# Expert rows summed into the residual inside the expert phase, by VectorE and GpSimd in turn

## What is computed

```python
x = x + xattn(ctx_768, layernorm(x), mask)
h = layernorm(x)
topk_idx, topk_w = route(h)                       # 4 of 32 experts per token
mixed  = sum over the 4 of  topk_w * down_e(silu(gate_e(h)) * up_e(h))
shared = shared_down(silu(shared_gate(h)) * shared_up(h))
x = x + mixed + shared
```

## Time and profile before

| | us |
|---|---|
| median of three runs (lowest, highest) | 1342.62 (1340.92, 1345.98) |
| the profiled execution | 1343.46 |
| its span, first to last instruction | 1341.5 |
| busy in the span: TensorE | 1298.0 (97%) |
| busy: ScalarE | 1011.6 (75%) |
| busy: VectorE | 972.0 (72%) |
| busy: GpSimd | 643.4 (48%) |

### The profile page before, as it was taken

How to read it: one execution, slowest core, us unless ns; L and a number is a source line. 1 busy time by engine, 2 the same in 40 slices (tenths; PEclk the granted TensorE clock), 3 DMA queues, 4 the chain that set the end, 5 groups by cost and what they waited for, 6 DMA issues and landing times.

```text
span 1341.5 us, 32944 instructions
## 1 busy us (share of the span) xinstructions
PE 1298.0 (97%) x8718; PEld 1043.2 (78%) x8718; DVE 972.0 (72%) x4498; ACT 1011.6 (75%) x2730; POOL 643.4 (48%) x724
## 2 busy tenths in 40 slices
PE   6999999999999999999979899999999999999997
PEld 4566676676676766766658799999999999988886
DVE  4578898888988988888887455555555555548887
ACT  4899999999999999999851566766776676653332
POOL 1113555555555555555455366666666666640000
PEclk8999999999999999999989899999999999999999
DMA  8234645535545445454487655555655555438896
GB/s 278 84 133 136 205 162 176 192 131 187 176 138 190 161 153 195 136 179 162 168 304 246 194 169 172 172 172 168 178 169 174 169 173 166 132 114 313 304 319 218
DMA packets 147714, 247.14 MB, mean 184 GB/s; under 512 B 24139, under 2 KB 110413, under 8 KB 146896
## 3 DMA queue, kind: packets, MB, share of 16 engines
q1 hardware_dynamic: 121472, 177.63, 41.3%
q0 software_dynamic: 26064, 67.42, 14.5%
HBM read 104.68 MB, written 119.96 MB: 167 GB/s over the span
## 4 chain that ended last, share of the span: by engine, by line
PE 63%; ACT 21%; DVE 9%; issue 5%; DMA 2%; SPq 0%; POOL 0%; ACTq 0%; DVEq 0%
PE psT L1033 10%; PE ps L1033 9%; PE psS L1043 9%; ACT arena L1168 6%; PE ps L916 6%; PE ps L1024 5%; PE ps L852 4%; ACT arena L1160 4%; PE psS L927 3%; PE psT L827 3%; PE psS L813 3%; PE psO L840 2%; ACT arena L1128 2%; ACT arena L1132 2%; ACT arena L1175 2%
## 5 line engine op out<-in xcount | busy, mean ns | idle before, releaser
L701 POOL DMA_INDIRECT expert_out<-pay,dest x287 | 282.1, 983 | 175.1 <-DVE dest L1878 157.4
L556 POOL DMA_INDIRECT lists<-pay,slot x168 | 174.3, 1037 | 187.7 <-PE psT L827 39.6
L1043 PE MATMUL psS<-arena,history 128*128 x574 | 171.8, 381 | 0.3 <-DVE history L1865 0.3
L1033 PEld LDWEIGHTS ps<-pad,hist_j 128*128 128x128 f32 x1152 | 152.1, 193 | 9.5 <-ACT pad L1315 2.1
L1033 PEld LDWEIGHTS psT<-pad 128*128 128x128 f32 x1144 | 151.0, 192 | 7.3
L1033 PE MATMUL ps<-pad,hist_j 128*128 128x128 f32 x1152 | 152.8, 276 | 1.9 <-ACT pad L1315 1.9
L1033 PE MATMUL psT<-pad 128*128 128x128 f32 x1144 | 151.6, 276 | 0.0
L1872 DVE TENSOR_SCALAR pay<-psS,dest 128x256 f32<-128x256 f32 x287 | 138.9, 484 | 1.6 <-PE psS L1043 1.5
L757 PE MATMUL ps<-arena 128*128 128x512 f32 x256 | 128.3, 624 | 2.6 <-ACT arena L1120 2.0
L556 POOL DMA_INDIRECT lists<-arena,slot x88 | 91.0, 1034 | 79.4 <-PE psT L827 20.6
L1168 ACT ACTIVATE arena<-arena,rden 128x256 f32<-128x256 f32 x256 | 109.1, 503 | 15.2 <-DVE rden L1466 15.1
(11 more groups left out here) (238 smaller groups left out, 3284.1 us busy)
## 6 DMA issues: line engine op xcount, KB each, us to landing
lists<-pad SPq DMA_DIRECT2D x72, 516.0 KB, 5.2
pay<-lists SPq DMA_DIRECT2D x287, 129.0 KB, 2.2
arena<-expert_out SPq DMA_DIRECT2D x32, 1024.0 KB, 7.1
pay<-pay SPq DMA_DIRECT2D x42, 384.0 KB, 3.6
x<-in_x SPq DMA_DIRECT2D x32, 256.0 KB, 4.7
out<-arena SPq DMA_DIRECT2D x31, 256.0 KB, 5.8
arena<-arena SPq DMA_DIRECT2D x20, 384.0 KB, 3.4
arena<-in_ctx SPq DMA_DIRECT2D x32, 192.0 KB, 4.6
```

What stands on the lines that cost most here:

```text
L556: pool.indirect_dma_start(lists, bass.IndirectOffsetOnAxis(ap=slots(u)[:, j, k:k + 1], axis=0), paid(u)[:, j, k, :], None).then_inc(scat[3 ...
L701: pool.indirect_dma_start(expert_out, bass.IndirectOffsetOnAxis(ap=dest[:, t % DESTS, 1:2], axis=0), yy[n], None, bounds_check=T * TOPK - ...
L1033: m = pe.matmul(ps[2 + n % 2][:, which * P:(which + 1) * P], w_now[1 - n % 2][:, k, which * I:(which + 1) * I], xsT[:, n % 2, k * P:(k + 1 ...
L1043: pe.matmul(dbank[n % 2][:, 0:D], hh[:, n % 4, :], w_dn[:, at(e, 1), :].rearrange("p a n -> p (a n)"), start=True, stop=True)\
```

## The change

In the expert phase, from tile 55 on, SP loads one piece for every two tiles: for one block of 128 tokens two of the four expert rows of each token (256 KB) into `side`, which has three buffers. VectorE adds the first row of the piece to `x1` in place (`add_first`, behind `weigh_result` of every second tile), and then GpSimd adds the second (`add_second`, behind a scatter). VectorE's add waits for the piece and for GpSimd's add of the piece before; GpSimd's waits for VectorE's of the same piece. 116 pieces cover the first 29 units (`IN_PHASE`); the last three are summed in the last stage as before, now into `x1`. The first eight units are stored during the expert phase; the others are stored from `x1` as their shared part is added, and `res` is gone. `n1T` is saved in HBM for all 32 units, and the last stage loads it into a ring of four instead of normalising and transposing again; `mr`, `norm_again`, `shared_turn` and `turned` are gone. The masks and `bo_b` move into `side`, which is free in the attention stage.

```diff
-ER_DEPTH = 4
+PIECES = 3
+IN_PHASE = 29
+PIECE_LOAD, PIECE_ADD = 55, 53
+N1T_RING = 4
...
+        side = sb("side", [P, PIECES, 2 * D])
+        mask_u8 = side[:, 0, 0:D].bitcast(u8).rearrange("p (a j n) -> p a j n", a=4, j=2)
+        mask_row = side[:, 0, D:2 * D].bitcast(bf16).rearrange("p (a j n) -> p a j n", a=2, j=2)
+        bo_b = side[:, 1, 0:D]
...
         def n1T_of(u):
-            flat = early_n1T[:, u] if u < EARLY else late_set[1]
+            flat = early_n1T[:, u] if u < EARLY else side[:, 0, :] if u == EARLY else n1T_ring[(u - EARLY - 1) % N1T_RING]
...
-                if (s + -2).exists() and s.n - 2 < EARLY:
+                if (s + -2).exists():
                     save_n1T(s + -2)
...
             load_experts(above, below_wo)
             spread_rows(Unit(UNITS // 2 - 1, 0))
-
+            save_n1T(Unit(UNITS // 2 - 1, 0))
 
             sp.wait_ge(y_done, NB)
             load_experts(below_wo, E)
             sp.wait_ge(scat[1], scattered(1, UNITS - 1))
             sp.dma_start(w_dn[:, 0:early], down[:, 0:early]).then_inc(weights_e, 16)
+            save_n1T(Unit(UNITS // 2 - 1, 1))
...
+            def load_piece(q):
+
+                u, b, half = q // 4, q // 2, q % 2
+                if q % 4 == 0:
+                    for n in range(SLOTS):
+                        sp.wait_ge(y_out[n], 16 * (E // SLOTS + 1 + u))
+                ge(sp, summed, q - PIECES + 1)
+                sp.dma_start(side[:, q % PIECES, :].rearrange("p (k n) -> p k n", k=2), er_d[:, b, 2 * half:2 * half + 2, :])\
+                  .then_inc(piece_in[q % PIECES], 16)
+
+            def store(u):
+                sp.dma_start(out_d[:, 2 * u:2 * u + 2, :], x1[:, 2 * u:2 * u + 2, :]).then_inc(stored, 16)
...
             for t in range(TILES):
                 load_tile(t, t % SLOTS)
...
+                q, odd = divmod(t - PIECE_LOAD, 2)
+                if odd == 0 and 0 <= q < 4 * IN_PHASE:
+                    load_piece(q)
+                done, odd = divmod(t - PIECE_LOAD - 17, 8)
+                if odd == 0 and 0 <= done < EARLY:
+                    sp.wait_ge(summed, 4 * (done + 1))
+                    store(done)
+
+            def load_late_n1T(u):
+                ge(sp, sgu_full, 2 * (u - N1T_RING + 1) if u > EARLY + N1T_RING else 0)
+                sp.dma_start(n1T_ring[(u - EARLY - 1) % N1T_RING], n1T_kept[u])\
+                  .then_inc(late_n1T_in[(u - EARLY - 1) % N1T_RING], 16)
+
+            sp.wait_ge(summed, 4 * IN_PHASE)
+            sp.dma_start(side[:, 0, :], n1T_kept[EARLY]).then_inc(first_n1T_in, 16)
+            sp.wait_ge(w_ready, TILES)
+            for u in range(EARLY + 1, EARLY + 1 + N1T_RING):
+                load_late_n1T(u)
             for n in range(SLOTS):
                 sp.wait_ge(y_out[n], 16 * ((TILES - 1 - n) // SLOTS + 1))
...
+            for v in range(IN_PHASE, UNITS):
+                sp.dma_start(er[:, v - IN_PHASE], er_d[:, 2 * v:2 * v + 2]).then_inc(er_in[v - IN_PHASE], 16)
+            for u in range(EARLY, UNITS - 1):
+                sp.wait_ge(sx_done, 2 * u + 2)
+                if u + N1T_RING + 1 < UNITS:
+                    load_late_n1T(u + N1T_RING + 1)
+                store(u)
...
+            def add_second(q):
+
+                pool.wait_ge(first_added, q + 1)
+                xb = x1[:, q // 2, :]
+                pool.tensor_tensor(xb, xb, side[:, q % PIECES, D:2 * D], ALU.add).then_inc(summed, 1)
+
             for t in range(TILES):
                 scatter_tile(t, t % SLOTS)
+                if (t + 3 - PIECE_ADD) % 2 == 0 and 0 <= t + 3 - PIECE_ADD < 2 * 4 * IN_PHASE:
+                    add_second((t + 3 - PIECE_ADD) // 2)
...
-            pe.wait_ge(yy_done, TILES)
-            shared_turn(EARLY)
+            pe.wait_ge(xst_ev, TILES)
+            pe.wait_ge(hh_done, TILES)
             for u in range(EARLY, UNITS + 1):
                 if u < UNITS:
                     shared_up(u, 0)
-                if u + 1 < UNITS:
-                    shared_turn(u + 1)
-                if u < UNITS:
                     shared_up(u, 1)
...
-                ge(act, n1T_saved, 16 * upto(u.n, EARLY))
+                ge(act, n1T_saved, 16 * u.n)
...
-                if old:
-                    u = run + -4
-                    dve.scalar_tensor_tensor(mr[:, at(2 * u.n, 2), 0], mv[:, 4:6, 0], -1.0, ra[:, 4:6], ALU.mult, ALU.mult)
-                    dve.tensor_copy(mr[:, at(2 * u.n, 2), 1:2], ra[:, 4:6].rearrange("p (j o) -> p j o", o=1))
...
+            def add_first(q):
+
+                dve.wait_ge(piece_in[q % PIECES], 16 * (q // PIECES + 1))
+                ge(dve, summed, q)
+                xb = x1[:, q // 2, :]
+                dve.tensor_tensor(xb, xb, side[:, q % PIECES, 0:D], ALU.add).then_inc(first_added, 1)
+
...
                 if t >= 1:
                     weigh_result(t - 1, (t - 1) % SLOTS)
+                if (t - PIECE_ADD) % 2 == 0 and 0 <= t - PIECE_ADD < 2 * 4 * IN_PHASE:
+                    add_first((t - PIECE_ADD) // 2)
```

More of the change, by code:

```diff
@@ L281, in build @@
         y_out = [sem(f"y_out{n}") for n in range(SLOTS)]
-        er_in = [sem(f"er_in{n}") for n in range(ER_DEPTH)]
-        nh, nt_full, nt_ev = sem("nh"), sem("nt_full"), sem("nt_ev")
+        piece_in = [sem(f"piece_in{n}") for n in range(PIECES)]
+        first_added, summed = sem("first_added"), sem("summed")
+        er_in = [sem(f"er_in{n}") for n in range(UNITS - IN_PHASE)]
+        first_n1T_in, late_n1T_in = sem("first_n1T_in"), [sem(f"late_n1T_in{n}") for n in range(N1T_RING)]
         sgu_full, ssg_done, sh_done = sem("sgu_full"), sem("ssg_done"), sem("sh_done")
         sd_full, sx_done = sem("sd_full"), sem("sx_done")
-        dC, dD, res_done = sem("dC"), sem("dD"), sem("res_done")
-        stored = [sem("stored0"), sem("stored1")]
+        dC, dD, er_done = sem("dC"), sem("dD"), sem("er_done")
+        stored = sem("stored")
         block = c.enter_context(nc.Block())
@@ L342, in wide @@
             return v.rearrange("(a n) -> a n", a=1).to_broadcast([P, v.shape[0]])
-        er = arena[:, 0:ER_DEPTH * 2 * TOPK * D].rearrange("p (a j k n) -> p a j k n", a=ER_DEPTH, j=2, k=TOPK)
-        used[0] = ER_DEPTH * 2 * TOPK * D
+        er = arena[:, 0:(UNITS - IN_PHASE) * 2 * TOPK * D].rearrange("p (a j k n) -> p a j k n", a=UNITS - IN_PHASE, j=2, k=TOPK)
+        used[0] = (UNITS - IN_PHASE) * 2 * TOPK * D
         esum, e2 = part(2, D), part(2, 2, D)
-        res = part(2, 2, D)
-        late_set = [part(2 * D) for _ in range(4)]
+        late_set = [part(2 * D) for _ in range(2)]
+        n1T_ring = [part(2 * D) for _ in range(N1T_RING)]
+        assert used[0] <= E * 2 * D
         first_n1T, above, below_wo = 6, 6 + EARLY, 17
@@ L496, in _ @@
             for j in range(2):
[L497 to L500, removed]
+                sp.wait_ge(sx_done, 2 * UNITS - 1 + j)
+                sp.dma_start(out_d[:, 2 * UNITS - 2 + j, :], x1[:, 2 * UNITS - 2 + j, :]).then_inc(stored, 16)
+            sp.wait_ge(stored, 16 * (UNITS + 1))
@@ L923, in shared_down @@
                     pe.wait_ge(pt_ev, NB - 1)
+                if u == EARLY:
+                    pe.wait_ge(yy_done, TILES)
                 for j in range(2):
@@ L1265, in _ @@
             in_order(step, UNITS)
-            def norm_again(u):
-                ge(act, nt_full, u - EARLY)
-                for j in range(2):
-                    b = 2 * u + j
-                    a = act.activation(n1_of(u)[:, j, :], x1[:, b, :], ACT.Identity,
-                                       bias=mr[:, b, 0:1], scale=mr[:, b, 1:2])
-                a.then_inc(nh, 1)
-            def turned(u):
-                act.wait_ge(nt_full, u - EARLY + 1)
-                ge(act, sgu_full, 2 * u)
-                act.activation(n1T_of(u).rearrange("p k n -> p (k n)"), psO[:, :], ACT.Copy).then_inc(nt_ev, 1)
             def shared_silu(u, mm):
@@ L1348, in _ @@
                     read_expert(t + 4)
-            act.wait_ge(dn_full, TILES)
-            norm_again(EARLY)
-            turned(EARLY)
             for u in range(EARLY, UNITS):
-                if u + 1 < UNITS:
-                    norm_again(u + 1)
                 shared_silu(u, 0)
-                if u + 1 < UNITS:
-                    turned(u + 1)
                 shared_silu(u, 1)
@@ L1918, in _ @@
                     add_shared(u - 1)
-                while summed < (u - EARLY + 1) * (UNITS + 1) // (UNITS - EARLY + 1):
-                    sum_experts(summed)
-                    sum_all(summed)
-                    summed += 1
-            sum_experts(UNITS - 1)
+                if u % 3 == 1 and u // 3 - 5 in range(UNITS - IN_PHASE):
+                    sum_experts(IN_PHASE + u // 3 - 5)
+            dve.wait_ge(er_done, UNITS - IN_PHASE)
             add_shared(UNITS - 1)
-            sum_last(UNITS - 1)
-            assert summed == UNITS - 1
 def kernel(x, ctx_768, mask_BxS2_bk0, L0_xattn_ln_x_g, L0_xattn_ln_x_b, L0_xattn_ln_l_g, L0_xattn_ln_l_b,
```

66 lines of the change are left out of this document (22 added, 44 removed).

## The result

The changed kernel takes 1361.15 us (median of 4 runs, 1359.51 to 1364.32) against 1343.59 for the kernel before (4 runs, 1340.92 to 1345.98): a ratio of 1.0134, 95% interval 1.0104 to 1.0164. It is slower by 17.6 us, where I had forecast 7. The measured time lies above the upper end of the range (1361), by less than the runs of one kernel differ among themselves. The profiled execution took 1364.32 us at a span of 1362.3, so it is 3.2 above the median; experiment 6 shows where such a difference can sit.

A forecast was written before the change was run, and what follows sets the result against it. It took TensorE as the bound before and GpSimd after the change: 1343.46 - 20.8 (last stage) + 28.8 (expert phase) - 0.8 (to a median) gave 1350.5, so 1350 us; range 1321 to 1361.

The forecast's parts named there:

- case A: Expert phase: GpSimd becomes the bound and the two adds meet the scatters; 1350 us, 1343 to 1360, chance 0.43.
- the loss of the expert phase: Expert phase: GpSimd becomes the bound after some 20 pairs, then TensorE loses 96 x 0.30 = 28.8 us.
- The lock: Expert phase: VectorE's two-input add holds GpSimd's next scatter until 0.12 us before the add's end; 0.19 us a pair.
- The seam (E): Between expert phase and last stage: unit 8's n1T loads only behind the last piece's `summed`; 0 to 4 us beside each case.
- The tail: Last stage and its start: 20.8 us less, with 5.19 us a unit and an end some 3 us behind TensorE.
- attention stage, the saves: Attention stage: saving n1T for all 32 units costs 0.
- the median of before: Kernel before: its profiled run of 1343.46 us was taken as 0.84 above a median of 1342.62.
- GpSimd's pair: Expert phase: two scatters, one add and the gaps cost GpSimd 3.21 us, against TensorE's 3.09.
- the slack predicted for it: Expert phase: VectorE's next add is due 1.9 us after GpSimd's add could end, so GpSimd may fall that far behind.
- The covers: Costs put at 0: piece loads, `load_piece`'s wait on SP, the n1T saves, and VectorE's 0.43 us add within 0.72 idle.
- B: Expert phase: GpSimd becomes the bound but the lock isn't met; 1333 us, 1325 to 1338, chance 0.27.
- C: Expert phase: GpSimd keeps pace, with an add of 0.63 us and no lock; 1322 us, chance 0.17.

The follow-up runs named there:

- experiment 6: The changed kernel with a second n1T buffer in the attention stage, so a copy doesn't wait for the save just before it: 1360.74 us.
- experiment 1: The changed kernel with VectorE's wait for GpSimd's previous add moved ahead of its copy of `dest` and its `weigh_result`: 1337.95 us, ratio 0.9957.
- experiment 2: The changed kernel with both adds on VectorE, the second one tile behind the first; GpSimd only scatters: 1323.19 us, ratio 0.9851.
- 5: The changed kernel with unit 8's n1T loaded earlier, into the third piece's buffer: 1357.06 us, ratio 1.0115.
- experiment 3: The changed kernel with the piece loads but no adds in the expert phase, loads paced by their own landing: 1323.07 us, ratio 0.9849.
- experiment 4: The changed kernel with GpSimd adding only 128 of the 256 columns of its row: 1327.69 us, ratio 0.9884.
- 8: The changed kernel with VectorE adding only the first 128 of the 256 columns of its row: 1348.32 us, ratio 1.0035.
- experiment 9: The changed kernel with GpSimd adding only 128 columns and VectorE's wait for GpSimd's previous add ahead of its copy of `dest`: 1324.41 us, ratio 0.9855.

## Why the prediction was wrong

The direction and the mechanism of case A held: GpSimd becomes the bound, VectorE's `add_first` waits for it, and that wait puts the add on the scatter. What failed were the sizes of two terms of the sum: the loss of the expert phase, in it the time for which the lock holds a scatter, and the seam, put at nothing because I had called it independent of the cases. The forecast had 1350.5, but its own terms give 1350.7; measured are 1361.2, so 10.5 us are to be found:

| term of the sum | predicted | measured | by |
|---|---|---|---|
| expert phase, loss | 28.8 | 33.8 | after, 1 and 2 |
| seam, unit 8's n1T and the clock behind it (E) | 0 | 4.1 | 5 |
| tail without that | -20.8 | -21.3 | 5 |
| attention stage, the saves | 0 | up to 0.8 | 3, 6 |
| the median of before | 1342.6 | 1343.6 | all sets of runs: 1343.0 to 1344.6 |

5.0 + 4.1 - 0.5 + 0.8 + 1.0 = 10.4. The attention stage's 0.8 is the rest of experiment 3 (1323.07, against 1343.59 - 21.3 = 1322.3), which is less than the runs can tell from nothing.

**GpSimd's pair.** The predicted 3.21 is 3.20, by two errors that nearly cancel: the add takes 0.75 us (I took 0.72 in a bound of 0.63 to 0.75), and it starts 0.01 behind the scatter and not 0.07. That is luck. The gaps of 0.30 and 0.16 held (0.30 and 0.17).

**The lock** is the first step that failed, with 5.0 us the larger one. The rule, held until 0.12 before the end of VectorE's operation, is what the runs show, but the earlier trace rows have 0.14 (563.31 - 562.68 - 1.47 + 0.98), so it was misread by 0.02. What I had wrong in the main was when VectorE's add starts: 0.05 behind GpSimd's, by estimate, where the rows have 0.11 (999.51 + 0.75 = 1000.26; 1000.37). 1000.37 + 0.42 - 0.12 - 1000.43 = 0.24 instead of 0.19. 0.05 us, 98 times, is 4.9 us, the size of this term's miss. (The pair without the lock is 0.01 shorter than predicted, and the sum had rounded its loss of 0.31 a pair down to 0.30; these two cancel.) VectorE began to wait after 17 pairs, so after 17 x 0.11 = 1.9 us, the slack predicted for it. The whole slack was less than the 3.0 taken: GpSimd's excess is 1.9 + 98 x 0.35 = 36.2 us, of which 33.8 reached TensorE, so 2.4.

**The seam (E)** is the second step that failed, with 4.1 us. I gave it "0 to 4 us beside each case" and took 0 for A. But E is not independent of A: it is A that makes GpSimd late, so that the last piece's `summed` comes at TensorE's end and not before. In experiment 2, without a late GpSimd, the first shared matmul follows at once; in the changed kernel and in experiments 1, 4, 6 and 8 it waits for 1.7 us or more. What that costs differs: by the tails 4.2 us in the changed kernel, 4.2 and 4.3 in experiments 6 and 8, where the clock falls behind the wait, but 1.9 and 2.4 in experiments 1 and 4, where it does not. In case A its upper end was due: with it the forecast had been 1355, and A's own range 1347 to 1364, which holds the result. I had let A's upper end carry 9 us for the length of a pair and nothing for E on top.

**The tail** held: 5.18 us a unit for 5.19, an end 2.6 us behind TensorE for the 3 predicted, and 21.3 us less for 20.8.

**The covers.** Costs set at nothing for VectorE's add (0.42, not 0.43), for the piece loads and for the saves were nothing. `load_piece`'s wait on SP, with the tile loads queued behind it, made VectorE wait for a tile 18 times, 10.1 us in all (there is no such wait in experiment 3, where `load_piece` doesn't wait for `summed`). It cost nothing, since GpSimd was late anyway: GpSimd's pairs around the two longest of these waits, of 1.2 us, last 3.42 to 3.45.

**The rivals.** B (no lock, 1333) is what experiment 1 made: 1337.95, with the seam's 1.9 us in it (1323.1 + 12.9 + 1.9 = 1337.9). C (GpSimd keeps pace, 1322) is what experiments 2 and 3 show as the time to be had: 1323. Both were well sized, and both needed another kernel: the changed one had neither an add of 0.63 nor its VectorE add elsewhere.

The Trainium skill (SBUF — State Buffer, "SBUF: two separate sides") calls the shared pair an exclusive lock that whoever starts first keeps for the whole instruction. The runs bear it out in part. VectorE's add holds the scatter when it starts ahead of it (0.24 us), but an add that starts 0.22 or 0.38 us into a scatter runs at its full speed (0.41 us), beside it, and does not wait for its end. Another operation of VectorE can be held that way. In experiment 4 a copy of `dest`, which takes 0.16 us otherwise, starts 0.31 us into a scatter (942.69, 0.97 long) and ends with it:
```profile
943.00 0.66 DVE L1881 COPY dest<-pay 128x2 int32<-128x2 int32 x1
```
Other copies that start within a scatter take 0.16 us, as the one at 1000.91 does; what decides there is not shown.

## What to carry to other kernels

Before work is given to an idle engine, add up the cycle of that engine, with its gaps, against the period of the bound: 0.11 us too much in 3.09 cost 13 us here, and the faster engine with its 0.72 us of idle time per tile took the same work for nothing. Where one engine's work can hold up the other's and the two also wait for each other, look at what starts in the same moment once one of them is late, since the wait itself lines them up, and the state can keep itself up. And price a seam's wait in each case for itself: an engine that has become the bound also delivers last.

## What the hardware showed that I had not expected

- A scatter of GpSimd was held by VectorE's two-input add only around its start. With the add 0.06 us ahead of it: 1.23 us (1.10 with the half add). With the add 0.22 or 0.38 us behind its start: 0.98 and 1.00.
- Contention can have two steady states in one execution: the same instructions at 3.09 us a pair, the tiles' pace, and at 3.17 (experiment 4). The slower one lasted for three pairs the first time and for all of the 30 pairs that were left the second time; with VectorE's wait moved it does not arise (experiment 9).
- GpSimd's `tensor_tensor` takes 0.47 us at 128x128, 0.75 at 128x256 and 1.27 at 128x512: by estimate from these three about 0.20 fixed and 0.27 for every 128 columns. VectorE's takes 0.29 and 0.42 for the first two, and 0.69 for the third.
- An idle time of 2.25 us cost TensorE nearly as much again in slow matmuls behind it (4.1 us in all, a granted clock of 0.83), while one of 2.12 us in experiment 4 cost no slow matmul (1.00).
- GpSimd stands idle for up to 3.1 us ahead of the scatters of tiles 113 and 219 in all eleven kernels, and the profile shows no cause. In the kernel before it costs nothing.
